# Last feed-forward: TensorE turns the quantised rows of the first product before the second down product of a turn

## The reference

```python
def _act_quant(x):                       # one scale per token
    scale = 127 / clip(max(abs(x), axis=-1), 1e-5)
    return clip(round(x * scale), -127, 127) / scale
def _bitlinear(x, w):                    # w rounded to -1, 0, 1 times its mean magnitude
    return einsum('bsi,oi->bso', _act_quant(x), _weight_quant(w))
t = _to_tokens(x)
h = square(relu(_bitlinear(_ln_t(t), w_up)))      # 512 -> 1024
t = t + _bitlinear(h, w_down)                     # 1024 -> 512
x = _from_tokens(t, x)
```

## Time and profile before

| | |
|---|---|
| timed runs of the kernel before | 1661.04, 1669.52 and 2396.83 us; median 1669.52 us |
| profiled execution, device time | 1656.12 us |
| its span, first to last instruction | 1654.0 us |
| the feed-forward in the profile, from its first wait for x to the end | 1476.06 to 1654 us |
| second down product (D1) of turn 0 and of turn 9, start | 1512.86 and 1625.95 us |
| TensorE clock granted from 1527.3 to 1627.8 us | 1.00 of full |

### The profile page before, as it was taken

One profiled execution on the slowest core, in us unless ns is written; L12 is line 12 of the kernel. 1 busy time (PEld: TensorE's weight loads), 2 busy tenths in 40 slices (PEclk: granted clock), 3 DMA queues, 4 the chain that ended last, 5 costly groups with the idle time before them and its releaser, 6 DMA issues. The chain is left out here.

```text
span 1654.0 us, 25471 instructions
## 1 busy us (share of the span) xinstructions
PE 1386.1 (84%) x8134; PEld 1144.5 (69%) x8134; DVE 982.9 (59%) x2091; ACT 709.1 (43%) x1162; POOL 606.6 (37%) x906
## 2 busy tenths in 40 slices
PE   5697999999483499999999994678899999927886
PEld 5596888888483378888888884658688888724443
DVE  5423788888456554445444433737378888846775
ACT  5322555555262133333233323512255555516886
POOL 1100365656412336555565532100036565640000
PEclk9799999999686589999999995579899999968999
DMA  7461122222294136555665526873111222130221
GB/s 243 125 174 39 39 67 76 67 67 66 93 308 155 41 109 117 104 124 110 138 123 97 118 28 182 285 249 95 39 46 60 76 67 76 58 115 23 87 64 57
DMA packets 105613, 173.88 MB, mean 105 GB/s; under 512 B 14864, under 2 KB 47168, under 8 KB 105540
## 3 DMA queue, kind: packets, MB, share of 16 engines
q1 hardware_dynamic: 83268, 128.86, 25.0%
q0 software_dynamic: 16384, 31.51, 11.1%
q10 hardware_dynamic: 5888, 12.59, 2.1%
HBM read 106.82 MB, written 66.10 MB: 105 GB/s over the span
## 5 line engine op out<-in xcount | busy, mean ns | idle before, releaser
L923 PE MATMUL g_y<-L_z,L_pt 128*128 128x192 f32 x1024 | 197.0, 336 | 1.6 <-ACT L_pt L1138 0.5
L1083 POOL TENSOR_TENSOR L_xr<-L_xr,L_lnb 128x192 f32<-128x192 f32 x128 | 105.4, 851 | 182.2 <-DMA L_xr<-x 96.2
L923 PEld LDWEIGHTS g_y<-L_z,L_pt 128*128 128x128 f32 x1024 | 166.7, 193 | 6.8 <-ACT L_pt L1138 6.8
L1456 POOL DMA_INDIRECT sums<-x_yo,x_places x64 | 103.0, 1609 | 141.3 <-ACT x_yo L1659 131.2
L1130 ACT ACTIVATE L_e<-g_s,L_nm 128x512 f32<-128x512 f32 x128 | 88.0, 688 | 79.0 <-DVE L_nm L971 77.4
L1090 POOL TENSOR_TENSOR L_t<-L_rstd 128x48 f32<-128x48 f32 x96 | 28.8, 300 | 222.7 <-DVE L_rstd L1025 217.7
L891 PE MATMUL g_z<-L_kw,L_xnT 96*128 96x192 f32 x512 | 91.8, 331 | 20.7 <-DVE L_v L1001 20.4
L1568 DVE TENSOR_TENSOR x_mid<-ex_g,x_sig 128x480 f32<-128x480 f32 (+1 forms) x48 | 31.4, 654 | 122.8 <-ACT x_sig L1650 122.8
L891 PEld LDWEIGHTS g_z<-L_kw,L_xnT 96*128 96x128 f32 x512 | 82.3, 189 | 29.9 <-DVE L_v L1001 29.9
L980 DVE SCALAR_TENSOR_TENSOR L_p<-L_e,L_rl,L_adj 128x512 f32<-128x512 f32 x128 | 99.1, 774 | 4.5
L971 DVE TENSOR_REDUCE L_nm<-g_s 128x1 f32<-128x512 f32 x128 | 87.6, 684 | 19.4 <-PE g_s L900 18.6
(11 more groups left out here) (343 smaller groups left out, 3566.1 us busy)
## 6 DMA issues: line engine op xcount, KB each, us to landing
L_xnT<-xn_rows SPq DMA_DIRECT2D x48, 384.0 KB, 3.4
x<-L_y SPq DMA_DIRECT2D x32, 384.0 KB, 2.8
xn_rows<-L_xnT SPq DMA_DIRECT2D x54, 192.0 KB, 4.0
L_xr<-in_x SPq DMA_DIRECT2D x24, 384.0 KB, 3.4
L_xr<-x SPq DMA_DIRECT2D x24, 384.0 KB, 3.8
L_raw<-xn_rows SPq DMA_DIRECT2D x16, 384.0 KB, 3.5
ff_xa<-x SPq DMA_DIRECT2D x12, 512.0 KB, 4.4
out_x<-ff_yo SPq DMA_DIRECT2D x16, 384.0 KB, 2.6
```

The lines of the kernel that those rows point to most:

```text
L923: last = nc.tensor.matmul(out, pt[k % 2][:, P * c:P * c + P], z[q][:, c, :], start=False, stop=(c == NK - 1))
L1083: last = nc.gpsimd.tensor_tensor(v_, v_, gain(s.lnb), ALU.add)
L1456: nc.gpsimd.indirect_dma_start(sums, row(places[e % 2][:, 1, t:t + 1]), yo[t % 4][:, :], None, compute_op=ALU.add).then_inc(sent[t % 4], 16)
```

## The change

On TensorE, `turn_q1(c + 2)` moves ahead of `go_down(c, 1)`. No instruction is added or taken away, and the lists of the other engines stay as they are.

```diff
                     if slab:
                         turn_slab(c + 3)
-                    if down:
-                        go_down(c, 1)
                     if quant:
                         turn_q1(c + 2)
                     if down:
+                        go_down(c, 1)
                         turn_out(c, 0)
```

## The result

The changed kernel takes 1647.74 us (median of six runs, 1638.15 to 1652.44) against 1668.13 for the kernel before; the ratio is 0.9878, with a 95% interval of 0.9831 to 0.9925. The forecast, 1652 us or 13.6 us off a base of 1665, is a ratio of 0.9918. The one run of 2396.83 us is left out of the ratio.

A forecast was written before the change was run, and what follows sets the result against it. Bound: a 12.57 us loop of ScalarE's list plus D1 ahead of Q. A turn falls to 11.21; 1.11 + 12.24 + 0.25 give 13.6 us off 1665.3, so 1652 us, range 1635 to 1666.

The forecast's parts named there:

- The bound: Feed-forward turn: ScalarE's list plus the time of D1, behind which ScalarE's next input Q stands; 12.57 us.
- The new loop: Feed-forward turn after the move: ten start-to-start joints, mostly TensorE's, with one wait, R0 to `lower_q2` to R1; 11.21 us.
- The sum: Feed-forward gain: 1.11 us at the first U0, 1.36 for each of nine more, 0.25 in turn 10; together 13.6.
- The cheapest end of the forecast: Feed-forward gain with the cheapest joints: 1.25 + 9 x 1.50 + 0.25, 15.0 us.
- The slack of Q: VectorE's loop through `quantise`: rows ready at 7.68 us after U0, against Q at 8.54; slack 0.86 us.
- The point from which the change loses: Lateness of VectorE's `quantise` that eats the whole gain of a turn: 0.86 + 1.36 = 2.2 us.
- ScalarE's own loop: Loop over ScalarE and TensorE, `lower_q2` of half 0 round to `lower_q2`: 11.00 us, slack 0.2, not deciding.
- ScalarE did not become full: Rival: ScalarE's gap closes, a turn falls to its busy time, 9.98 us; gain 25.9, so 1639 us; chance 0.05.
- The joints at full length: Rival: TensorE goes on only after the whole of X, Q and F0; turn 11.57, 1655.5 us; chance 0.17.
- Q waiting for VectorE: Rival: late `quantise` holds Q, D1, F0 and the next U0; at 3.0 us lateness 1673 us; chance 0.05.
- The marks in the profile: Values expected in the feed-forward timeline after: turn near 11.2, hole about 0.5, R1's wait about 1.0, D1 1.45 after X.
- three signs of failure: Prediction wrong if Q starts over 1.2 after X, D1 waits over 0.1 for `scale_out`, or the clock leaves 1.00.

The follow-up runs named there:

- an early `scale_out`: Kernel before, with `scale_out` of half 0 moved ahead of `round_squares` of half 0 on ScalarE; turn 12.41 us, block 177.22 us.
- the first measurement: Changed kernel against the kernel before: medians 1647.74 us against 1668.13, ratio 0.9878.
- the second: Changed kernel timed again, five rounds against the kernel before: 1649.88 us against 1663.27, ratio 0.9921.
- one extra pass: Changed kernel with one more VectorE pass over tn ahead of quantise's first instruction, into an unread tile; turn 11.47 us, block 170.36 us.

## Why the prediction was right

*The bound* was the loop `scale_out`, D1, Q, `lower_q1` and ScalarE's list. Shown: a group put into it (F0, 0.43) lengthens the turn by its own length, and taking D1 out leaves 11.01. What the prediction did not see is the second loop, 12.41 with an early `scale_out`, so close under it; as D1 and Q are in both, the change shortened both. Its list of TensorE's holes also left out 0.45 ahead of F1, which lies between R0 and R1 and so inside a joint that it counted.

*The new loop* has the ten joints of the forecast, and eight of them came as taken, to 0.02: from the timeline after, D1 to F0 1.73, U0 to R0 1.72, to `lower_q2` 0.65, to R1 1.26, to U1 0.44, to D0 1.73, to X 1.73, Q to D1 0.45. The two others were too dear: X to Q is 0.87 (1.0 taken) and F0 to U0 0.44 (0.5). The sum is 11.02 where 11.21 was forecast. That is the term that was mis-sized, and it was mis-sized toward the durations that the rows print: eight float32 transposes show 1.04, but the next group starts 0.87 after them.

*The sum.* A turn gains 1.56, not 1.36, in nine turns 1.8 us more. The first U0 gains 1.30 on its X, not 1.11, by the same two joints (4.78 after X before, 3.48 now). With both the 13.6 become 15.6, and 15.5 and 15.3 were measured (177.94 - 162.40, and - 162.68). The cheapest end of the forecast was 15.0, which is passed because X to Q came below the 0.95 that was taken as its least. The totals are no test of this: the medians differ by 20.4 us in the first measurement and by 13.4 in the second, and that the latter is so near to 13.6 is chance.

*The slack of Q* was put at 0.86 and is 0.67; 0.13 of the difference is the shorter X, which brings Q earlier, and the other 0.06 is the time from the end of `quantise` to the start of a Q that waits for it (1589.72 to 1589.78 with one extra pass). The point from which the change loses was put at 2.2 us of lateness and lies at about 2.27. ScalarE's own loop, put at 11.00, is indeed close below: with the joints as measured it is 10.94, since D1 starts 0.90 after `scale_out` of half 0 (1579.33 to 1580.23) and needs 0.82. A later `scale_out` shows at once: with R1 3.31 after R0 instead of 1.91 (U1 ahead of it), D1 waited for ScalarE's list and the turn went to 11.89.

*The rivals.* ScalarE did not become full, as its busy share of 92% shows, 10.13 us a turn; the chain on TensorE stands above that. The rule of the Trainium skill that this rival rested on, from Perfetto Trace Analysis, sections Identifying the Most-Contended Engine and Optimization Strategy, points to the right engine and to its large gap. The trace agrees only so far: with Q ahead of X the last gap ahead of `lower_q1` was gone, but ScalarE idled 1.15 ahead of `lower_q2`, and the turn was 0.21 longer by Q's wait for VectorE. The joints at full length were refuted by 0.87 and 0.44. Q waiting for VectorE is real, and needs more than 0.67 us of lateness, which this kernel doesn't have.

*The marks in the profile* were 11.2, 0.5, 1.0 and 1.45 for the turn, the hole ahead of `lower_q1`, the wait of R1 and D1 after X; they came as 11.01, 0.43, 0.85 and 1.32. Of the three signs of failure two did not show: Q starts 0.87 after X, and the granted clock stays at 1.00. The third, D1 waiting more than 0.1 for `scale_out`, shows in the last of the ten turns, turn 9, which has no X between D0 and Q:

```profile
1624.20 1.89 PE L2022 MATMUL ff_d<-s_wdn,ff_q2s 128*128 128x512 bf16 x8 [0.42 <-ACT ff_od L2211]
```

This wait was 1.08 before, so it took nothing from the gain; the prediction's sign did not allow for the turn without X.

*The base.* 1652 us was 4 us above the first median and 2 above the second; the missing 1.9 us of gain and the scatter of the blocks ahead are both in that.

## What to carry to other kernels

Where no engine is full, write down the loop of waits that the turn is, engine by engine from start to start, and check that it adds up to the turn; then move the small group that another engine waits for ahead of a large one whose result is needed later. Before doing so, read how long its data have been ready: that slack is what the move spends. Take joints from start to start, not from printed durations, and compare the block that changed, not the whole span, where the blocks ahead scatter by more than the change is worth.

## What the runs showed of the hardware that was not expected

The blocks ahead of the feed-forward, the same instructions in every kernel, ended, by the first load of the feed-forward, between 1476.06 and 1497.84 us over the thirteen profiled executions, a scatter of 21.8 us, while the feed-forward block of the changed kernel repeated to 0.3 (162.40, 162.68). The two ends of the scatter go with the mean granted clock of their executions, 0.905 and 0.886; those between fall in nearly the same order. That the clock is the cause was not tried.

Eight 16-bit transposes hold TensorE for 0.44 to 0.46 us from start to start, and eight float32 ones for 0.87, though their rows show 0.61 and 1.04. This is at a granted clock of 1.00.

In the start-up of the block the clock still moves. The U0 of turn 0, behind a wait of 1.21 in most kernels, took 3.27 to 3.59 us at a granted clock of 0.50 to 0.55 in ten of the thirteen executions, 1.90 at 1.00 in two and 2.15 at 0.87 in one. So two kernels whose turns are alike can differ by some 1.5 us there.
